# One attention and expert layer on one core: projection tiles of a sequence spread over its four quarters, and the natural pass 27 places ahead of the scores

## The reference, cut to what matters

```python
# x: (8, 512, 256) float32; 16 heads of 16; 8 experts with 1024 hidden units; capacity 129
k, q, v = (x @ W.T split in heads, times 256 ** -0.5  for W in (W_key, W_query, W_value))
scores = where(causal, q @ k.T * 16 ** -0.5, -inf)
a = softmax(scores) @ v                       # heads joined again
x = layernorm(x + (a @ W_proj.T) * 256 ** -0.5)
gate, tokens = top_k(softmax(x @ router_w.T) transposed, 129)      # experts choose their tokens
y = (gelu(x[tokens] @ w1 + b1) @ w2 + b2) * gate                   # for each of the 8 experts
x = layernorm(x + scatter_add(y, tokens))
```

## Time and profile before

| | |
|---|---|
| runs | 901.45, 902.26, 900.26 us; median 901.45 |
| the profiled execution | 902.58 us, of which its span is 900.8 us |
| mean granted TensorE clock of the span | 0.962 of full speed |
| busy over the span | TensorE 820.8, VectorE 601.5, ScalarE 533.2, GpSimd 473.5 us |
| score unit 0 of sequence 0, 3, 4, 6, 7 issued at | 61.6, 208.7, 259.0, 359.2, 401.9 us |
| first expert matmuls | 467.3 us |

### The profile page before, as it was taken

How to read it: one execution, slowest core, us unless ns; L and a number is a source line. 1 busy time by engine, 2 the same in 40 slices (tenths; PEclk the granted TensorE clock), 3 DMA queues, 4 the chain that set the end, 5 groups by cost and what they waited for, 6 DMA issues and landing times.

```text
span 900.8 us, 17159 instructions
## 1 busy us (share of the span) xinstructions
PE 820.8 (91%) x5876; PEld 613.8 (68%) x5876; DVE 601.5 (67%) x2059; ACT 533.2 (59%) x1048; POOL 473.5 (53%) x642
## 2 busy tenths in 40 slices
PE   4788999999999999998778999999999999999990
PEld 3544454454645454434268999999999999999990
DVE  4488777878788788899858845546464544546464
ACT  2237667667575767676647445555565656555554
POOL 6448565656656565345558356435344435436253
PEclk9669999999999999999789999999999999999995
DMA  4653434536352424520343124335252333523158
GB/s 140 221 182 110 133 110 154 154 106 183 124 151 99 153 90 151 188 72 2 111 174 108 30 43 64 84 83 147 36 130 48 77 95 53 136 31 59 20 146 263
DMA packets 89990, 100.52 MB, mean 112 GB/s; under 512 B 8624, under 2 KB 83376, under 8 KB 89776
## 3 DMA queue, kind: packets, MB, share of 16 engines
q1 hardware_dynamic: 72448, 77.92, 27.0%
q0 software_dynamic: 12800, 16.92, 11.3%
q10 hardware_dynamic: 4656, 4.59, 1.5%
HBM read 65.38 MB, written 33.62 MB: 110 GB/s over the span
## 4 chain that ended last, share of the span: by engine, by line
PE 73%; DVE 13%; ACT 6%; issue 3%; DMA 2%; POOL 1%; ACTq 0%; SPq 0%; POOLq 0%; DVEq 0%
PE y_ps L1357 21%; PE h_ps L1343 19%; PE av_ps L792 7%; PE st_ps L760 5%; DVE n_ps L624 5%; PE n_ps L775 5%; PE stage_ps L809 4%; PE stage_ps L851 3%; PE stage_ps L817 3%; PE tp_ps L1316 2%; ACT pt L522 1%; DVE nmax L624 1%; ACT res L504 1%; PE stage_ps L842 1%; PE stage_ps L801 1%
## 5 line engine op out<-in xcount | busy, mean ns | idle before, releaser
L624 DVE CUSTOM_DVE_ANT_0 n_ps<-n_ps,tri 128x512 f32<-128x512 f32 (+3 forms) x512 | 238.5, 520 | 75.8 <-PE n_ps L775 74.1
L522 ACT ACTIVATE pt<-st_ps 128x512 f32<-128x512 f32 x320 | 184.4, 602 | 64.3 <-PE st_ps L760 49.2
L1357 PE MATMUL y_ps<-w_parts,h_hi 128*128 128x256 f32 (+1 forms) x1152 | 215.2, 281 | 2.1 <-issue 1.5
L1177 ACT ACTIVATE g<-h_ps,b 128x384 f32<-128x384 f32 (+1 forms) x192 | 104.2, 543 | 162.2 <-PE h_ps L1343 134.8
L1357 PEld LDWEIGHTS y_ps<-w_parts,h_hi 128*128 128x128 f32 (+1 forms) x1152 | 172.4, 177 | 6.0 <-issue 1.8
L1149 POOL DMA_INDIRECT acc<-y,tok_no x64 | 102.9, 1608 | 139.8 <-DVE y L1292 129.7
L1343 PE MATMUL h_ps<-tt_hi,w_parts 128*128 128x384 f32 (+1 forms) x768 | 169.7, 323 | 3.6 <-issue 2.0
L1278 DVE TENSOR_TENSOR h_lo<-g,h_hi 128x384 fp32r<-128x384 f32 (+1 forms) x176 | 90.4, 514 | 118.7 <-ACT h_hi L1182 101.4
L451 POOL TENSOR_SCALAR_AFFINE_SELECT pt<-pt 128x256 f32<-128x256 f32 (+1 forms) x320 | 110.6, 363 | 106.8 <-ACT pt L522 106.0
L1357 PE MATMUL y_ps<-w_parts,h_lo 128*128 128x256 f32 (+1 forms) x576 | 161.5, 280 | 0.0
L760 PE MATMUL st_ps<-w_parts 99*128 99x512 bf16 (+3 forms) x512 | 126.4, 309 | 15.7 <-ACT pt L522 14.2
(11 more groups left out here) (192 smaller groups left out, 1079.6 us busy)
## 6 DMA issues: line engine op xcount, KB each, us to landing
w_parts<-part_d SPq DMA_DIRECT2D x192, 128.0 KB, 2.7
w_raw<-in_w SPq DMA_DIRECT2D x16, 1024.0 KB
part_d<-w_raw SPq DMA_DIRECT2D x96, 128.0 KB, 2.1
w_raw<-in_xt SPq DMA_DIRECT2D x8, 512.0 KB, 3.8
res<-in_x SPq DMA_DIRECT2D x8, 512.0 KB, 4.5
x<-res SPq DMA_DIRECT2D x8, 512.0 KB, 3.2
acc<-res SPq DMA_DIRECT2D x8, 512.0 KB, 5.2
fin<-acc SPq DMA_DIRECT2D x4, 512.0 KB, 4.3
```

The costliest lines, as they stand in the source:

```text
L522: nc.scalar.activation(pt[:, slot % PT_RING, n % UP, :], st_ps[at % ST_RING][:, :], ACT.Exp, scale=S_SCALE).then_inc(exp_done, 1)
L624: ins = nc.vector.tensor_tensor_reduce(out=src[:, h, :], in0=src[:, h, :], in1=mask, scale=-1.0, scalar=-BIG_NEG, op0=ALU.add, op1=ALU.min ...
L1177: nc.scalar.activation(g[:, at % G_RING, 0:cols], h_ps[at % H_RING][:, 0:cols], ACT.Gelu, bias=b1[:, e, n:n + 1]).then_inc(g_done, 1)
L1357: ins = nc.tensor.matmul(y_ps[at % Y_RING][0:rows, 0:C], x[:, q % 2, m, toks], w[e % 2][:, m, :], start=i == 0, stop=i == len(terms) - 1)
```

## The change

Two constants and the tables of the order change; no operation is added or taken away.

- The natural pass runs 27 places ahead, not 30, and its 44 units are dealt over the 40 places of a sequence in one run (two units at places 2, 12, 22, 32 instead of 9, 19, 29, 39).
- `nmcut` and `nm` move with it by three places: of the first eight heads from places 30 and 34 to 33 and 37, of the others from 11 and 14 to 14 and 17. At place 17 `nm` stands behind a q/k tile. The first sequence's move from (-1, 3, 0) to (-1, 3, 3) and (-1, 3, 5).
- The q/k tiles of sequence i+2 move from places 2, 10, 17, 22 to 9, 17, 26, 30; its v tiles from 25, 26, 27, 28 to 32 and 39 and to places 0 and 1 of the following sequence; its `split` from place 35 of the sequence before to place 2. `onorm` 2 moves from place 8 to place 0.
- The first two sequences keep the old places of `qk`, `v` and `split` (`FIRST_STAGES`).

```diff
--- before.py
+++ after.py
@@ -50,44 +50,58 @@
 
 
 STAGES = (
+    (0, 0, 'onorm', -1, 2),
+    (0, 0, 'v', 1, 2),
+    (0, 1, 'v', 1, 3),
     (0, 1, 'stack', 1, 1),
     (0, 2, 'res', 0, 0),
-    (0, 2, 'qk', 2, 0),
-    (0, 8, 'onorm', -1, 2),
-    (1, 0, 'qk', 2, 1),
+    (0, 2, 'split', 2, 0),
+    (0, 9, 'qk', 2, 0),
+    (1, 7, 'qk', 2, 1),
+    (2, 6, 'qk', 2, 2),
+    (3, 0, 'qk', 2, 3),
+    (3, 2, 'v', 2, 0),
+    (3, 9, 'v', 2, 1),
     (1, 0, 'onorm', -1, 3),
-    (1, 1, 'nmcut', 0, 1),
-    (1, 4, 'nm', 0, 1),
+    (1, 4, 'nmcut', 0, 1),
+    (1, 7, 'nm', 0, 1),
     (1, 5, 'ot', -1, 0),
     (1, 6, 'ot', -1, 1),
-    (1, 7, 'qk', 2, 2),
     (1, 8, 'proj', -1, 0),
     (1, 9, 'proj', -1, 1),
     (2, 0, 'proj', -1, 2),
     (2, 1, 'proj', -1, 3),
     (2, 1, 'stack', 2, 0),
-    (2, 2, 'qk', 2, 3),
     (2, 4, 'onorm', 0, 0),
     (2, 3, 'rstd', -1, 0),
-    (2, 5, 'v', 2, 0),
-    (2, 6, 'v', 2, 1),
     (2, 7, 'logit', -1, 0),
-    (2, 7, 'v', 2, 2),
-    (2, 8, 'v', 2, 3),
-    (3, 0, 'nmcut', 1, 0),
+    (3, 3, 'nmcut', 1, 0),
     (2, 9, 'lexp', -1, 0),
     (2, 9, 'x1', -1, 0),
     (3, 0, 'x1', -1, 1),
     (3, 1, 'x1', -1, 2),
     (3, 2, 'x1', -1, 3),
     (3, 2, 'score', -1, 0),
-    (3, 4, 'nm', 1, 0),
+    (3, 7, 'nm', 1, 0),
     (3, 3, 'onorm', 0, 1),
+)
+
+
+FIRST_STAGES = (
+    (0, 2, 'qk', 2, 0),
+    (1, 0, 'qk', 2, 1),
+    (1, 7, 'qk', 2, 2),
+    (2, 2, 'qk', 2, 3),
+    (2, 5, 'v', 2, 0),
+    (2, 6, 'v', 2, 1),
+    (2, 7, 'v', 2, 2),
+    (2, 8, 'v', 2, 3),
     (3, 5, 'split', 3, 0),
 )
-
-
-NAT_LEAD = 3
+FIRST = 2
+
+
+NAT_LEAD = 27
 HH = H // 2
 HALF = T // 2
 B_AT = 64
@@ -111,16 +125,17 @@
 
     for i in range(-3, B + 1):
         for g in range(4):
-            nat_b, nat_0 = (4 * i + g + NAT_LEAD) // 4, (4 * i + g + NAT_LEAD) % 4 * N_QUARTER
             for k in range(10):
-                if (i, g, k) == (-1, 3, 0):
+                if (i, g, k) == (-1, 3, 3):
                     yield "nmcut", 0, 0
+                if (i, g, k) == (-1, 3, 5):
                     yield "nm", 0, 0
                 if 0 <= i < B:
                     yield "st", i, (2 * g) * UP + k
+                nat_b, at = divmod(40 * i + 10 * g + k + NAT_LEAD, 40)
                 if 0 <= nat_b < B:
-                    for n in range(N_QUARTER * k // 10, N_QUARTER * (k + 1) // 10):
-                        yield "nat", nat_b, nat_0 + n
+                    for n in range(NU * at // 40, NU * (at + 1) // 40):
+                        yield "nat", nat_b, n
                 group = i * GROUPS + g - 1
                 if k in AV_PLACES and 0 <= group < B * GROUPS:
                     yield "av", group, AV_PLACES.index(k)
@@ -130,7 +145,10 @@
                 if (i, g, k) == (-1, 2, 0):
                     yield "fold", 0, 0
                 for gg, kk, stage, ahead, n in STAGES:
-                    if (gg, kk) == (g, k) and 0 <= i + ahead < B and (i, stage, n) not in STARTED:
+                    if (gg, kk) == (g, k) and (FIRST if stage in ("qk", "v", "split") else 0) <= i + ahead < B and (i, stage, n) not in STARTED:
+                        yield stage, i + ahead, n
+                for gg, kk, stage, ahead, n in FIRST_STAGES:
+                    if (gg, kk) == (g, k) and 0 <= i + ahead < FIRST and (i, stage, n) not in STARTED:
                         yield stage, i + ahead, n
                         if (i, stage, n) == (-1, "qk", 1):
                             yield "stack", 1, 0
```

## The result

The changed kernel takes 941.34 us (median of 4 runs, 940.64 to 943.24) against 900.86 for the kernel before in the same comparison (4 runs, 900.18 to 902.26): a ratio of 1.0452, 95% interval 1.0435 to 1.0468. The forecast was 904.5 with a range of 894 to 911. Lines of kernel.py from the edited tables on have moved by 18: score units are issued in L778, natural units in L793, av in L810, q/k tiles in L827, v tiles in L835, the transposes of the maxima in L855, their copy in L584.

The account below looks back on a forecast made before the run. TensorE's queue was taken to set the 50.3 us period. Per sequence 2.1 us won and 2.5 lost gave +0.4, +2.4 over six; with +0.7 at the ends, +3.1 in all: 904.5 us, range 894 to 911.

Parts of the forecast that it names:

- Gain 0.9, the wait for the cut: Place 14: TensorE's 1.23 us wait before the transposes for VectorE's late cut shrinks; 0.9 us won per middle sequence.
- Gain 1.2, spreading: Tiles at places 39, 0, 1 and 9 cover TensorE's waits for exponentials; 1.2 us won per middle sequence.
- Loss 0.9, the first eight heads' rows: Transposes at place 37 land rows late for unit 0; new TensorE wait of 0.9 us per middle sequence.
- Loss 1.2, the other eight heads' rows: Transposes at place 17 behind a q/k tile land rows late for unit 20; new wait of 1.2 us per sequence.
- Loss 0.4, the split: Place 2: the split's 1.05 us ScalarE copy stands right behind two v tiles' copies; 0.4 us net lost per sequence.
- The ends: First and last sequences together: -2.3 - 1.7 + 2.7 + 2.0 = +0.7 us.
- First score unit: Start: fewer natural units precede it, so it goes at about 59.3 instead of 61.62; -2.3 us.
- Tail: End: natural units saved in front come back in the stretch where VectorE is busy 25.15 of 26.70 us; +2.7 us.
- Sequence 0: Two v tiles fall away to sequence 1; -1.7 us.
- Sequence 6: Two new waits for rows without a q/k tile to hide in, 1 us each, one in sequence 7; +2.0 us together.
- Rival 1: Faster: spreading wins 2.7 us a sequence instead of 1.2, giving 895.5 us; chance 0.32.
- Rival 2: Slower: the cut at place 33 is held by GpSimd's tile subtractions, +1.2 us a sequence, giving 912 us; chance 0.17.

Follow-up runs that it names:

- Experiment 7: Kernel before with only the other eight heads' transposes moved from place 14 to 16, their cut left at place 11: 903.59 us, ratio 1.0013.
- experiment 1: Changed kernel with the natural pass again 30 places ahead and nmcut and nm at their old places, tiles still spread: 903.39 us, ratio 1.0012.
- experiment 2: Kernel before with only the lead of 27 (cuts at places 14 and 33, transposes at 17 and 37), tiles at old places: 954.18 us, ratio 1.0581.
- experiment 10: Changed kernel with only the first eight heads' rows turned earlier, at place 35 instead of 37: 919.59 us, ratio 1.0193.
- 4: Changed kernel with both turns of the rows earlier, at places 35 and 16 instead of 37 and 17: 913.03 us, ratio 1.0129.
- experiment 6: Changed kernel with only the other eight heads' rows turned earlier, at place 16 instead of 17: 936.40 us, ratio 1.0392.
- experiment 8: Changed kernel, rows turned at places 35 and 16, each quarter's double natural unit at its place 9 instead of 2: 906.47 us, ratio 1.0045.
- 11: Changed kernel, rows turned at places 35 and 16, double natural units at place 9 of each quarter, SyncE's stores held until rows landed: 905.08 us, ratio 1.0033.
- 12: Changed kernel, lead back at 30, cuts at places 32 and 13, rows turned at 35 and 16, pairs at place 9, stores held: 904.54 us, ratio 1.0028.
- experiment 5: Changed kernel with SyncE's stores of sequence b held until the first eight heads' rows of sequence b+2 have landed: 937.57 us, ratio 1.0395.

## Why the prediction was wrong

The side was the likelier one (slower, 0.49), and the mechanism that the prediction named, TensorE waiting for the rows in front of units 0 and 20, is the one that decided. The size was off by a factor of 13: 3.1 us were forecast, 40.5 came. By its own steps, per middle sequence:

- **Gain 0.9, the wait for the cut.** 0. Experiment 7: what place 14 gives back, 0.74 us, place 15 takes. The error was to price an idle stretch by the wait named in front of it, without asking what VectorE is late with next.
- **Gain 1.2, spreading.** 0, together with the split (experiment 1, ratio 1.0012). The waits for exponentials rose, from 33.5 to 46.2 us in five sequences of the changed kernel. Beside late rows the new places do help (experiment 2).
- **Loss 0.9, the first eight heads' rows.** This is the step that failed: 3.25 us of period (55.91 in the change, 52.66 in experiment 10). Three terms of it were mis-sized. The landing: I took 2.1 us by the nearest row, a store of 128 KB, and called the smaller size a reason to take the lower one; it is 2.65 alone, and 3.3 to 4.8 at the place to which the change moves it, where SyncE's stores and stack reads run. The forecast said that SyncE's new order costs nothing, as nobody waits for its transfers; a transfer of ScalarE's queue did. TensorE's flow: I had unit 0 ready 2.85 us behind the transposes (257.15 to 260.0), and it was 2.1 (216.98 to 219.1), as the 2.24 us I had started from held waits for exponentials; I had named that, and allowed for half. With the measured landing and flow the forecast's wait of 0.7 us becomes 2.8 in front of sequence 3 (2.99 in the trace; 3.3 in the mean of sequences 2 to 6). And the clock, 1.1 us in the mean, which the forecast took as unchanged. Wait and clock together are 4.4 us; the difference of 3.25 is smaller because experiment 10 still has 0.5 us of this wait and 0.6 elsewhere.
- **Loss 1.2, the other eight heads' rows.** Right in size: 1.3 (52.66 to 51.35, experiments 10 and 4; 0.8 from the change to experiment 6, which lost its clock more often). In part it is luck, as sequence 3 of the changed kernel shows:

```profile
242.04 0.30 PEld L827 LDWEIGHTS stage_ps<-xt_hi,w_hi 128*128 128x128 f32 x2 [0.20 <-ACT o_t L590]
...
248.00 0.10 PEld L778 LDWEIGHTS st_ps<-w_parts 99*128 99x128 bf16 x1 [1.10 <-DMA w_parts<-nmt]
```

There the rows are in place 5.96 us behind the tile's issue, not 5.5, and TensorE is at unit 20 after 4.86, not 4.3: two errors of half a microsecond cancel in the wait of 1.1.

- **Not in the sum: the pair of natural units.** 0.9 (51.35 to 50.42, experiments 4 and 8). The new places of the pairs were known; what they meet on VectorE was put at nothing, without a reason.
- **Loss 0.4, the split.** Not told apart; it is within experiment 1's 0.
- **The ends.** First score unit: 61.02 (59.3 forecast, 61.62 before). It scatters by 2 us: the kernel before and experiment 7, the same up to there, have 61.62 and 63.81. The ten kernels with a lead of 27 have a mean of 62.3, the four with 30 of 63.1, so not -2.3 but about -0.8, less than the scatter. Tail, from unit 0 of sequence 7 to the first expert matmul: +2.7 forecast. It is +4.6 between 11 and 12, and 67.5 against 64.1 us in the means of the same ten and four traces, so the term holds; but in the changed kernel's own trace it is 64.9 where the kernel before has 65.4, the shortest of the ten, so the forecast's sign of 3 us more is not to be seen there. Sequence 0: -1.7 forecast, +3.0 came, as the rows' waits begin there; with these waits gone (experiment 8) it is 0.3 shorter than before. Sequence 6: +2.0 forecast for both late sequences, +6.8 came in this one, of which the earlier first rows of experiment 10 give back 4.0.

So 0.4 a sequence became 5.6, and the terms above give 5.5 of it: 2.1 of gains that were none less 0.4 for the split, 2.4 more for the first rows, 0.1 for the others, 0.9 for the pairs. Of the 40.5 us, by the kernels' differences to the kernel before: 23.3 are the first rows (40.5 to 17.2; of it some 5 to 7 the clock, an estimate from 1.2 to 1.5 us for each of four or five falls in sequences 1 to 6), 6.6 the other rows, 5.2 the pairs, 2.7 the rest that held stores give back, and 2.7 remain, whose place is not shown.

**The rivals.** Rival 1 fell with experiment 1. Rival 2's sign is there and its effect is not: at place 33 the cut takes 1.67 us (268.16 to 269.83), 0.70 of it the first cast of 32 columns.

```profile
268.16 0.70 DVE L672 CAST nm<-nmax 128x32 bf16<-128x32 f32 x1
...
267.66 1.16 POOL L480 TENSOR_TENSOR w_raw<-w_raw 128x512 bf16<-128x512 f32 x1
```

The cast ends 0.04 us behind GpSimd's subtraction (268.82). That agrees with the rule of the Trainium skill ("SBUF — State Buffer", SBUF: two separate sides) that one of the two engines blocks while the other has the shared port pair. But the cut was done 1.7 us before the transposes of place 37 (271.50). The range was too narrow because each unknown was bounded by itself: no case in it held a transfer stretched by its neighbours, and none a second price behind a wait.

## What to carry to other kernels

When a step whose result crosses a DMA is moved towards its user, price the landing at its new place, with what the other queues move there, and by a row of the same path and size or with a wide upper end. Ask of every idle stretch of TensorE that a change makes, if it is as long as those here (2.2 to 4.3 us), whether the clock survives it, and of every wait that it removes what the engine named is late with next. If a rounding formula deals work over places, write out the places it gives before and after, and look at each new place on every engine that takes a share of that work.

## What was not expected of the hardware

- A transfer of 24 KB within SBUF, issued by ScalarE, takes 2.65 us to the unit that waits for it when nothing else moves (experiment 5, 218.57 to 221.22), and 3.3 to 4.8 us beside SyncE's queue. The Trainium skill ("DMA: Bandwidth & Descriptors", Anatomy of one DMA — SWDGE (gpsimd) path) gives a fixed cost of about 2.0 us, roughly constant, for transfers that GpSimd issues; no run here shows that path alone, and for this transfer of ScalarE's queue the measured time decides: it is longer, and it is not constant.
- Idle stretches of 2.2 to 4.3 us on TensorE were followed by about 3 us at half clock (0.50 from 221.20 to 224.50 in experiment 5, 0.50 from 166.10 in the changed kernel), but not each time: behind the 2.99 us at 221.90 of the changed kernel the clock was 1.00. Each fall cost 1.2 to 1.5 us. Repeating a v tile's matmuls, which nobody needs, through the wait made the kernel 5.6 us faster (7.1 against the kernels before beside them).
